# Two-layer conditional residual block on one core: TensorE's row loop begins at step 4, and two VectorE operations go behind a seven-product pair

## The chip, the cores and the metric

One core of one Trainium2 chip. The metric is device time in microseconds of one execution. Engines: PE (TensorE, matrix products; PEld is its weight loads), DVE (VectorE), ACT (ScalarE), POOL (GpSimd), SP (SyncE, which issues the DMAs).

## The reference

`x` is [8, 512, 256] in float32, `cond` [8, 8]. Layer 0 adds to each batch row the gated MLP of a shared expert and the two best of 8 experts (by `cond`, weights from a softmax); layer 1 adds a linear map with a low-rank part that depends on the row. Cut to what matters:

```python
def mlp(x, gate, up, down):                  # 256 -> 1024 -> 256
    return (gelu(x @ gate) * (x @ up)) @ down
w, sel = top_k(softmax(cond), 2);  w = w / w.sum()
x = x + sum(w[b, s] * mlp(x[b], *expert[sel[b, s]]) for s in range(2)) + mlp(x[b], *shared)
x = x + x @ W_base.T + b_base + 2 * sum_e cond[b, e] * (x @ As[e].T) @ Bs[e].T
```

## The kernel before

**Arithmetic.** Every float32 operand of PE is kept as two tensors: a high part (ACT writes it, `take_hi`, line 1086) and a remainder, the low part (DVE writes it, `take_lo`, line 1432). A product is three matmuls (high by high, high by low, low by high; `product`, line 757).

**Stages.** First the shared expert's MLP for all tokens (to about 250 us), then the routed experts and layer 1, one batch row after the other: `row(b, ...)` for b = 0 to 7 on each engine. A row has K = 16 steps, two for each 256 inner columns (a pair of steps) of the two experts. Pairs 1, 3, 5 and 7 (steps 2 and 3, 6 and 7, 10 and 11, 14 and 15; in row 0 only from step 6 on) form their gate and up parts by seven products of half the columns (`seven_products` on PE, `ex_seven` on DVE, from line 1691) in place of eight; they need sums of blocks of the weights and of the tokens, which POOL makes. The other pairs are whole steps.

**PE in a row.** At a whole step: gate (6 matmuls of 512 columns), up (6), the down part of two steps before (6). At a pair of seven: 42 matmuls of 256 columns, then two down parts (12 of 512). The last two down parts of a row are done in steps 0 and 1 of the next. Steps 4 and 8 carry layer 1 of the row before (12 matmuls) and the fold of the low-rank weights (6). The seventh product waits for `ex_v_done`, which DVE's line 1697 gives.

**DVE in a row.** At a whole step: gelu times up (line 1757), what is due at this step, the low part of the result, and more of what is due. At a pair of seven, `ex_seven`: lines 1697 and 1699 (add to copies of products), 1688, 1706, 1708, 1688 twice, then two low parts. What is due at a step is set by hand: `split_at` (the low part of a whole pair's weights, 1536 columns, line 1432), `sums_at` (of the sums of the weights), and constants. `T_STEP` = 13: `split_sums_x`, the low part of the next row's token sums. `W_EFF_STEP` = 9: line 1794 adds the folded weights, of PSUM, to the rest. Both come at a whole step just ahead of a pair of seven (14, 10). At step 14 the low part of the weights of the next row's pair 1 follows the seven.

**Order and loops.** Each engine runs its queue in program order, with semaphores between. On PE, ACT, DVE and SP row 0 is written out, rows 1 to 6 are a loop of three turns with two rows each, and row 7 is written out; POOL's loop has one row a turn. So each of PE, ACT and DVE jumps back twice, between rows 2 and 3 and between rows 4 and 5, and all of them at the same place of the program, the end of a row.

Of the kernel before, what the change touches and what calls it, by code (L numbers as in the profile page):

```python
# [5 lines left out]
ALU = mybir.AluOpType  # L6
# [29 lines left out]
def cond_resid_kernel(nc, x, cond, skill_gate, skill_up, skill_down, shared_gate, shared_up,  # L36
                      shared_down, w_base, b_base, lora_a, lora_b, out):
    B, S, H = x.shape
    E, _, I = skill_gate.shape
    R = lora_a.shape[1]  # L40
    HC = H // P
# [4 lines left out]
    K = TOP_K * IC  # L46
# [8 lines left out]
    COEF_STEP = 13  # L55
    FOLD_STEP = 8
    W_EFF_STEP = 9
    W_EFF_LO_STEP = 12
    X_STEP = 8
    T_STEP = 13  # L60


# [6 lines left out]
    with ExitStack() as ctx:  # L69
# [22 lines left out]
        w_id = sb("w_id", [P, HC * H])  # L92
# [25 lines left out]
        ps_misc = acc[1]  # L118
# [633 lines left out]
        def _(pe):  # L752
# [261 lines left out]
                    last = pe.transpose(ps_misc[1][:, o * P:(o + 1) * P], b_nat[:, o, :], ident[:])  # L1014
                last.then_inc(turned_w, 1)

            def row(b, par, first):
                pe.wait_ge(x_ready, b + 1)
                for k in range(K):
                    if k % 2 == 0:  # L1020
                        pe.wait_ge(weights_ready, b * (TOP_K * PAIRS) + k // 2 + 1)
                    if k // 2 in sevens_of(first):
                        if k % 2 == 0:
                            seven_products(b, par, k, SEVEN.index(k // 2), first)
                            if k == 2:

                                pe.wait_ge(x1_done, b * 2)
                            down(b, k - 2, first)
                            down(b, k - 1, first)
                        continue  # L1030

                    behind_seven = k // 2 - 1 in sevens_of(first) or (k < 2 and not first)
                    st = seventh(b, k, first)
                    if behind_seven:
                        if k % 2 == 0:
                            pe.wait_ge(ex_mul, 3 * st - 2)
                        else:
                            pe.wait_ge(ex_u1_done, st)
                    elif k >= 2:
                        pe.wait_ge(gelu_done, whole(b, k - 1, first))  # L1040
                    elif k == 0:
                        pe.wait_ge(sh_mul, 4 * (NU - 1) + 1)
                    else:
                        pe.wait_ge(u1_done, 2 * (NU - PAIRS))
                    project(par, k, ring[k % 2], GATE).then_inc(gate_done, 1)
                    if behind_seven:
                        pe.wait_ge(ex_c_done, 2 * st - 1 + k % 2)
                    elif k >= 2:
                        pe.wait_ge(mul_done, whole(b, k - 1, first))
                    else:  # L1050
                        pe.wait_ge(c_done, 4 * (NU - PAIRS) - 1 + k)
                    project(par, k, ring[2 + k % 2], UP).then_inc(up_done, 1)
                    if k == 1 and first:
                        shared_down_part(NU - 1, 0)
                        shared_down_part(NU - 1, 1)
                    if k < 2 and not first:

                        down(b - 1, K - 2 + k, False)
                    if k == 2:
                        pe.wait_ge(acc0_out, 2 * Q)  # L1060
                    if k >= 2:
                        down(b, k - 2, first)
                    if k == L1_STEP and not first:
                        layer1(b - 1)
                    if k == CONST_STEP and first:
                        pe.wait_ge(acc1_out, 2 * Q)
                        turn_constants()
                    if k == FOLD_STEP:
                        if first:
                            pe.wait_ge(w_turned, 1)  # L1070
                        else:
                            pe.wait_ge(o_ready, b * 2)
                        fold(b)

            row(0, 0, True)
            with pe.Fori(0, (B - 2) // 2) as i:
                row(i * 2 + 1, 1, False)
                row(i * 2 + 2, 0, False)
            row(B - 1, 1, False)
            down_last()  # L1080
            layer1_last()

# [345 lines left out]
        def _(dve):  # L1428
# [249 lines left out]
            def split_sums_x(b, par):  # L1678
                dve.wait_ge(ex_t_hi, b + 1)
                take_lo(sums_x(par, 1), t_tmp, sums_x(par, 0)).then_inc(ex_t_ready, 1)  # L1680
# [40 lines left out]
            def row(b, par, first, last):  # L1721
# [3 lines left out]
                def split_pair(pr):  # L1725
                    if pr < 2 * PAIRS:
                        split_routed(b, pr // PAIRS, pr % PAIRS, pr in sevens_of(first))
                    elif not last:
                        split_routed(b + 1, 0, pr - 2 * PAIRS, pr - 2 * PAIRS in SEVEN)

                def rest_of_x():
                    dve.wait_ge(x_hi, b + 2)
                    take_lo(x_cur(1 - par, 1), xf, x_cur(1 - par, 0)).then_inc(x_ready, 1)

                for k in range(K):
                    s = k // IC
                    if k // 2 in sevens_of(first):
                        if k % 2 == 0:
                            ex_seven(b, par, k, SEVEN.index(k // 2))
                            if k in split_at:  # L1740
                                split_pair(split_at[k])
                            if k == 2:
                                layer1_lo(b - 1)
                        continue
                    dve.wait_ge(gelu_done, whole(b, k, first) + 1)
                    dve.wait_ge(up_done, whole(b, k, first) + 1)
                    if k % 2 == 0 and (k // 2 - 1 in sevens_of(first) or (k == 0 and not first)):

                        dve.wait_ge(inner_ready, b * K + k)
                    if k == 0:  # L1750
                        if first:
                            dve.wait_ge(coef_done, 2)
                            V.tensor_copy(coef_now[:, 0, :], coef[:, 0, :]).then_inc(coef_ready, 1)
                        dve.wait_ge(coef_ready, b + 1)
                    if first and k < 2:
                        dve.wait_ge(sh_inner_hi, 4 * (NU - 1) + k + 1)
                    V.scalar_tensor_tensor(out=inner[k % 2], in0=gelu[k % 2], scalar=coef_now[:, par, s:s + 1],  # L1757
                                           in1=ring[2 + k % 2][:], op0=ALU.mult, op1=ALU.mult)\
                        .then_inc(mul_done, 1)

                    if k == L1_STEP + 1 and not first:
                        turn_output(b - 1)
                    if k == 1 and not first:

                        layer1_sum(b - 1)
                    if k == 4 and first:
                        split_sums_x(0, 0)
                    if k in sums_at:
                        split_sums_w(b, sums_at[k])
                    if k in split_at:  # L1770
                        split_pair(split_at[k])
                    if k == (BW_STEP if first else 0):
                        dve.wait_ge(bw_hi, b + 1)
                        V.scalar_tensor_tensor(out=bw_s[1], in0=b_t[:], scalar=coef_now[:, par, TOP_K:TOP_K + 1],
                                               in1=bw_s[0].bitcast(F32), op0=ALU.mult, op1=ALU.subtract)\
                            .then_inc(bw_ready, 1)
                    dve.wait_ge(inner_hi, b * K + k + 1)
                    take_lo(inner_s[1][:, k % 4, :], inner[k % 2], inner_s[0][:, k % 4, :])\
                        .then_inc(inner_ready, 1)
                    if first and k == 1:  # L1780
                        acc1_to_stage(Q - 1)
                    if k == L1_STEP and not first:
                        split_sums_w(b, 1)
                        split_pair(4)
                    if k == CONST_STEP and first:
                        layer1_constants()
                    if k == T_STEP and not last:
                        split_sums_x(b + 1, 1 - par)
                    if k == X_STEP and not last:
                        rest_of_x()  # L1790
                    if k == W_EFF_STEP:
                        dve.wait_ge(fold_done, b + 1)
                        dve.wait_ge(w_id_done, HC)
                        V.tensor_tensor(w_eff[:], ps_misc[0][:], w_id[:], ALU.add).then_inc(w_eff_done, 1)
                    if k == COEF_STEP and not last:
                        V.tensor_copy(coef_now[:, 1 - par, :], coef[:, b + 1, :]).then_inc(coef_ready, 1)
                    if k == W_EFF_LO_STEP:
                        dve.wait_ge(w_eff_hi, b + 1)
                        take_lo(w_eff_s[1], w_eff[:], w_eff_s[0]).then_inc(w_eff_ready, 1)
# [57 lines left out]
```

## Time and profile before

| | us |
|---|---|
| median of 3 runs | 809.85 |
| the three runs | 806.36, 809.85, 4542.35 |
| the profiled execution, whole time | 810.33 |
| its span, first to last instruction | 808.5 |
| mean granted TensorE clock, share of full | 0.995 |
| PE busy | 796.3 |
| DVE busy | 694.0 |
| ACT busy | 486.4 |
| POOL busy | 316.6 |

Times of the trace count from the span's start. "Idle before" names what ended an engine's idle time; "issue" means that nothing which the profile shows was waited for. Waits of some tenths appear with the weight loads and not with the matmuls, since a matmul still runs while the next load waits. The rows 1 to 7 of the batch begin at 317.94, 385.54, 455.64, 524.98, 595.02, 664.37 and 731.95 us by PE's first product.

### The profile page before, as it was taken

The numbers are of one execution on the slowest core, as the hardware profiler recorded it, in microseconds if no ns is written. First come the engines' busy times: TensorE is split into PE (matmuls) and PEld (weight loads), VectorE is DVE, ScalarE is ACT, GpSimd is POOL, SyncE is SP. The second block draws the span as 40 slices with busy tenths as digits, with TensorE's granted clock in tenths as the row PEclk, the third lists the DMA queues.
The fourth block names the chain that finished last, engine by engine and source line by source line (L and its number), as shares of the span: only waits on it lengthen the run. The fifth ranks groups of instructions, "written<-read, shape, count | busy, mean of one in ns | idle before, by whom it ended". The sixth has DMA issues, their size and how long they took to land.

```text
span 808.5 us, 13442 instructions
## 1 busy us (share of the span) xinstructions
PE 796.3 (98%) x4140; PEld 685.2 (85%) x4140; DVE 694.0 (86%) x916; ACT 486.4 (60%) x743; POOL 316.6 (39%) x308
## 2 busy tenths in 40 slices
PE   9999999999999999999999899999989999999998
PEld 7888888888888888888888789888878888898887
DVE  4886987987877899989989798998978999899886
ACT  6564554654654556666666566666756666675663
POOL 1441321321110773465246346425624632653520
PEclk9999999999999999999999999999999999999999
DMA  7340521303214422353163245316324522632400
GB/s 207 78 115 15 155 66 21 112 0 105 92 39 123 149 81 79 112 163 118 40 195 100 78 128 150 100 63 173 116 84 126 148 79 88 176 100 68 130 2 27
DMA packets 120160, 80.86 MB, mean 100 GB/s; under 512 B 62480, under 2 KB 115472, under 8 KB 120080
## 3 DMA queue, kind: packets, MB, share of 16 engines
q1 hardware_dynamic: 120080, 79.88, 33.9%
q8 instruction: 39, 0.64, 0.3%
q14 instruction: 41, 0.34, 0.1%
HBM read 67.28 MB, written 12.58 MB: 99 GB/s over the span
## 4 chain that ended last, share of the span: by engine, by line
PE 92%; DVE 5%; issue 2%; ACT 0%; POOL 0%; DVEq 0%; POOLq 0%; ACTq 0%
PE ps_ring L757 57%; PE ps_acc L757 33%; DVE inner_lo L1432 1%; DVE xc L1432 1%; DVE wide L1432 1%; PE ps_ring L877 1%; DVE post L1697 1%; DVE post L1757 0%; PE ps_acc L965 0%; DVE sh_dn L1432 0%; PE ps_acc L985 0%; PE ps_acc L871 0%; PE ps_ring L775 0%; DVE stage L1831 0%; ACT post L1322 0%
## 5 line engine op out<-in xcount | busy, mean ns | idle before, releaser
L757 PE MATMUL ps_ring<-xc,wide 128*128 128x512 f32 (+1 forms) x1938 | 421.9, 366 | 6.4 <-issue 4.6
L757 PEld LDWEIGHTS ps_ring<-xc,wide 128*128 128x128 f32 x1938 | 340.8, 189 | 68.2 <-issue 5.5
L1086 ACT CAST inner_hi<-post 128x512 fp32r<-128x512 f32 x192 | 117.7, 620 | 111.5 <-DVE post L1757 38.8
L757 PE MATMUL ps_acc<-inner_hi,wide 128*128 128x512 f32 x504 | 171.3, 390 | 0.0
L1432 DVE TENSOR_TENSOR inner_lo<-post,inner_hi 128x512 fp32r<-128x512 f32 x192 | 152.5, 802 | 8.6 <-ACT inner_hi L1086 5.7
L1089 ACT ACTIVATE post<-ps_ring 128x512 f32<-128x512 f32 (+1 forms) x125 | 67.8, 545 | 93.5 <-PE ps_ring L757 92.1
L757 PEld LDWEIGHTS ps_acc<-inner_hi,wide 128*128 128x128 f32 x504 | 94.9, 188 | 19.2
L757 PE MATMUL ps_acc<-inner_lo,wide 128*128 128x512 f32 x252 | 98.5, 391 | 0.0
L1089 ACT ACTIVATE post<-post 128x256 f32<-128x256 f32 (+1 forms) x98 | 53.8, 563 | 65.0 <-DVE post L1706 46.5
L637 POOL TENSOR_TENSOR post<-post 128x512 f32<-128x512 f32 x24 | 31.0, 1292 | 135.4 <-DVE post L1484 135.4
L757 PE MATMUL ps_acc<-inner_hi,sh_dn 128*128 128x512 f32 x256 | 83.9, 389 | 0.0
L1757 DVE SCALAR_TENSOR_TENSOR post<-post,coef_now,ps_ring 128x512 f32<-128x512 f32 x66 | 49.3, 746 | 30.1 <-PE ps_ring L757 29.1
L1432 DVE TENSOR_TENSOR wide<-raw,wide 128x1536 fp32r<-128x1536 f32 (+3 forms) x38 | 67.9, 1786 | 7.4 <-ACT wide L1086 7.4
L708 POOL TENSOR_TENSOR post<-post 128x256 f32<-128x256 f32 x62 | 44.5, 739 | 75.3 <-DVE post L1699 75.1
L716 POOL TENSOR_TENSOR post<-post 128x256 f32<-128x256 f32 x32 | 41.3, 1319 | 55.6 <-DMA post<-sh_scratch 55.6
L757 PE MATMUL ps_ring<-xc 128*128 128x256 f32 x456 | 62.3, 283 | 0.0
L1432 DVE TENSOR_TENSOR wide<-xbuf,wide 128x1536 fp32r<-128x1536 f32 x32 | 59.6, 1863 | 0.0
L757 PEld LDWEIGHTS ps_ring<-xc 128*128 128x128 f32 x456 | 58.1, 192 | 0.1
L757 PEld LDWEIGHTS ps_acc<-inner_hi,sh_dn 128*128 128x128 f32 x256 | 48.1, 188 | 10.0
L1086 ACT CAST wide<-raw 128x1536 fp32r<-128x1536 f32 (+3 forms) x40 | 52.3, 1308 | 4.8 <-DMA raw<-_L_cond_shared_gate_dram 3.7
L757 PEld LDWEIGHTS ps_acc<-inner_lo,wide 128*128 128x128 f32 x252 | 47.6, 189 | 8.8
L1432 DVE TENSOR_TENSOR xc<-stage,xc 128x1024 fp32r<-128x1024 f32 (+1 forms) x44 | 52.3, 1197 | 0.0
(128 smaller groups left out, 1040.4 us busy)
## 6 DMA issues: line engine op xcount, KB each, us to landing
raw<-n_L_cond_skill_gate_dram SPq DMA_DIRECT2D x32, 256.0 KB, 3.0
raw<-in_L_cond_skill_up_dram SPq DMA_DIRECT2D x32, 256.0 KB, 3.5
raw<-n_L_cond_skill_down_dram SPq DMA_DIRECT2D x32, 256.0 KB, 3.8
xbuf<-n_L_cond_skill_gate_dram SPq DMA_DIRECT2D x32, 256.0 KB, 3.0
xbuf<-in_L_cond_skill_up_dram SPq DMA_DIRECT2D x32, 256.0 KB, 3.5
xbuf<-n_L_cond_skill_down_dram SPq DMA_DIRECT2D x32, 256.0 KB, 3.7
xt_scratch<-xbuf SPq DMA_DIRECT2D x8, 512.0 KB, 3.1
sh_scratch<-stage SPq DMA_DIRECT2D x8, 512.0 KB, 2.7
```

The source lines that it names most:

```text
L637: G.tensor_tensor((g_t if part == GATE else i_t)[3], v57, u1, ALU.add).then_inc(c22_done, 1)
L708: last = G.tensor_tensor(ex_v[:, half], ex_v[:, half], ex_u1[:, half], ALU.add)
L716: done = G.tensor_tensor(base[:, part], base[:, part], xf[:, part], ALU.add)
L757: last = pe.matmul(dst, left_[a], right_[b], start=start and n == 0, stop=stop and n == len(PASSES) - 1, skip_group_check=adds)
L877: pe.transpose(ring[3][:, 0:P], ident[:], ident[:])
L1086: return nc.scalar.copy(dst, src)
L1089: return nc.scalar.activation(dst, src, ACT.Gelu_apprx_tanh)
L1432: return V.tensor_tensor(dst, src, hi.bitcast(F32), ALU.subtract)
L1697: V.tensor_tensor(ex_v, ring[3][:], ex_v, ALU.add).then_inc(ex_v_done, 1)
L1757: V.scalar_tensor_tensor(out=inner[k % 2], in0=gelu[k % 2], scalar=coef_now[:, par, s:s + 1], in1=ring[2 + k % 2][:], op0=ALU.mult, op1=AL ...
```

## The change

PE's loop is turned by four steps: the first four steps of row 1 are written out ahead of it, and the loop's last piece is the first four steps of the row after. The wait on `x_ready` goes to step 0 inside `row`. On DVE, `split_sums_x` moves from step 13 to behind `ex_seven` of step 14, ahead of the weights' remainder there; `fold_sum` (line 1794 with its waits) moves in row 0 from step 9 to behind `ex_seven` of step 10, and stays at step 9 in the other rows. ACT, POOL and SP are as before.

```diff
+    W_EFF_FIRST_STEP = 10
+    TURN_STEP = 4
...
-            def row(b, par, first):
-                pe.wait_ge(x_ready, b + 1)
-                for k in range(K):
+            def row(b, par, first, steps=range(K)):
+                for k in steps:
+                    if k == 0:
+                        pe.wait_ge(x_ready, b + 1)
...
             row(0, 0, True)
+            row(1, 1, False, range(TURN_STEP))
             with pe.Fori(0, (B - 2) // 2) as i:
-                row(i * 2 + 1, 1, False)
+                row(i * 2 + 1, 1, False, range(TURN_STEP, K))
                 row(i * 2 + 2, 0, False)
-            row(B - 1, 1, False)
+                row(i * 2 + 3, 1, False, range(TURN_STEP))
+            row(B - 1, 1, False, range(TURN_STEP, K))
...
+                def fold_sum():
+                    dve.wait_ge(fold_done, b + 1)
+                    dve.wait_ge(w_id_done, HC)
+                    V.tensor_tensor(w_eff[:], ps_misc[0][:], w_id[:], ALU.add).then_inc(w_eff_done, 1)
...
                             ex_seven(b, par, k, SEVEN.index(k // 2))
+                            if k == T_STEP + 1 and not last:
+                                split_sums_x(b + 1, 1 - par)
+                            if k == W_EFF_FIRST_STEP and first:
+                                fold_sum()
                             if k in split_at:
                                 split_pair(split_at[k])
...
-                    if k == T_STEP and not last:
-                        split_sums_x(b + 1, 1 - par)
...
-                    if k == W_EFF_STEP:
-                        dve.wait_ge(fold_done, b + 1)
-                        dve.wait_ge(w_id_done, HC)
-                        V.tensor_tensor(w_eff[:], ps_misc[0][:], w_id[:], ALU.add).then_inc(w_eff_done, 1)
+                    if k == W_EFF_STEP and not first:
+                        fold_sum()
```

## Rows read from the trace of the kernel before

**Rows 1.** The page, part 1: busy time of each engine.

```profile
PE 796.3 (98%) x4140; PEld 685.2 (85%) x4140; DVE 694.0 (86%) x916; ACT 486.4 (60%) x743; POOL 316.6 (39%) x308
```

**Rows 2.** Waits of PE and PEld: us in total, times, longest us.

```profile
PE ps_ring L757 <- issue: 4.6, 2, 2.4
...
PEld ps_ring L757 <- DVE post L1697: 3.7, 8, 1.7
```

**Rows 3.** Windows, rows 1, 2, 3, 7: length, busy (instructions), clock, DMA, GB/s.

```profile
317.94:385.54 67.60, 67.49 (x380) 59.22 (x378) 62.63 (x76) 44.30 (x64) 32.98 (x32) 1.00 0.40 118
385.54:455.64 70.10, 67.63 (x380) 59.03 (x378) 64.72 (x78) 44.90 (x65) 31.70 (x32) 1.00 0.38 114
455.64:524.98 69.34, 69.22 (x379) 60.45 (x379) 60.17 (x73) 43.65 (x63) 32.87 (x32) 0.98 0.39 115
...
731.95:799.17 67.22, 67.22 (x379) 59.15 (x378) 55.94 (x72) 40.21 (x61) 21.19 (x24) 1.00 0.19 52
```

**Rows 4.** Windows about PE's first jump and in row 0, same columns.

```profile
452.90:456.40 3.50, 1.15 (x5) 0.67 (x4) 3.26 (x4) 0.64 (x2) 0.00 (x0) 1.00 0.01 5
456.40:459.81 3.41, 3.41 (x9) 2.63 (x8) 0.00 (x0) 1.74 (x3) 0.00 (x0) 0.50 0.04 12
...
296.00:299.40 3.40, 1.92 (x15) 1.68 (x14) 3.40 (x6) 0.87 (x2) 1.97 (x3) 1.00 0.52 162
```

**Rows 5.** Timeline of PE where rows 2 and 3 begin: start, us, what.

```profile
385.54 2.88 PE L757 MATMUL ps_ring<-xc,wide 128*128 128x512 f32 x12
...
452.90 0.39 PE L757 MATMUL ps_acc<-inner_hi,wide 128*128 128x512 f32 x1
455.64 4.61 PE L757 MATMUL ps_ring<-xc,wide 128*128 128x512 f32 x12 [2.35 <-issue]
```

**Rows 6.** Timeline of DVE, row 1, steps 13 and 14.

```profile
380.03 1.21 DVE L1432 TENSOR_TENSOR xc<-stage,xc 128x1024 fp32r<-128x1024 f32 x1
...
381.24 0.68 DVE L1697 TENSOR_TENSOR post<-ps_ring,post 128x512 f32<-128x512 f32 x1
```

**Rows 7.** Timeline of PEld, the seventh product of step 14 in row 1.

```profile
381.97 0.78 PEld L757 LDWEIGHTS ps_ring<-sh_dn,wide 128*128 128x128 f32 x6 [0.31 <-DVE post L1697]
```

**Rows 8.** Timeline of DVE and PEld, row 0, steps 9 and 10.

```profile
296.91 0.68 DVE L1794 TENSOR_TENSOR w_eff<-ps_acc,w_id 128x512 f32<-128x512 f32 x1
297.51 0.67 DVE L1697 TENSOR_TENSOR post<-ps_ring,post 128x512 f32<-128x512 f32 x1
...
298.24 0.77 PEld L757 LDWEIGHTS ps_ring<-xc,wide 128*128 128x128 f32 x6 [1.68 <-DVE post L1697]
```

**Rows 9.** Timeline of DVE, then PEld, row 2, steps 0 to 4.

```profile
388.69 0.75 DVE L1757 SCALAR_TENSOR_TENSOR post<-post,coef_now,ps_ring 128x512 f32<-128x512 f32 x1
...
392.61 0.75 DVE L1757 SCALAR_TENSOR_TENSOR post<-post,coef_now,ps_ring 128x512 f32<-128x512 f32 x1 [0.49 <-PE ps_ring L757]
...
396.77 0.68 DVE L1697 TENSOR_TENSOR post<-ps_ring,post 128x512 f32<-128x512 f32 x1
...
402.45 1.22 DVE L1432 TENSOR_TENSOR sh_dn<-post,sh_dn 128x1024 fp32r<-128x1024 f32 x1
...
397.89 0.79 PEld L757 LDWEIGHTS ps_ring<-xc,wide 128*128 128x128 f32 x6
...
401.25 2.68 PEld L757 LDWEIGHTS ps_ring<-xc,wide 128*128 128x128 f32 x12
```

**Rows 10.** Instruction packets begun in 450.9:451.3, then in 454.3:455.4 (packets, MB, DMA share).

```profile
q8 instruction: 2, 0.03, 58.3%
...
q14 instruction: 2, 0.02, 4.3%
```

**Rows 11.** Timeline of DVE and ACT, the end of row 2 and row 3's step 0.

```profile
454.49 1.75 DVE L1432 TENSOR_TENSOR wide<-raw,wide 128x1536 fp32r<-128x1536 f32 x1
460.54 0.75 DVE L1757 SCALAR_TENSOR_TENSOR post<-post,coef_now,ps_ring 128x512 f32<-128x512 f32 x1 [4.30 <-PE ps_ring L757]
...
458.07 0.60 ACT L1089 ACTIVATE post<-ps_ring 128x512 f32<-128x512 f32 x1 [4.22 <-PE ps_ring L757]
```

## The prediction, made before the changed kernel was run

> **What bounds the kernel now.** I read the page first, then PE's waits and the row-by-row windows, then the timeline where those showed time missing. PE is busy for 796.3 of 808.5 us and DVE for 694.0 [rows 1], so PE is the bound, and only its idle or slowed time can be won. PE's own list of waits is short: two "issue" waits, 4.6 us together, and little else. The weight loads, which show shorter waits too, list 8 waits on DVE's line 1697, 3.7 us in all [rows 2]. The windows say which rows pay. Row 7, the last, takes 67.22 us, row 1 67.60, row 2 70.10 and row 3 69.34; rows 4, 5 and 6 repeat rows 2, 3 and 1 within 0.1 us [rows 3]. The work is the same in all but the last row's end, so three losses stand over 67.22:
> - 0.37 us in every row but the last (67.60 - 67.22, taken as the same 0.37 in all six rows from 1 to 6);
> - 2.50 us more in rows 2 and 4 (70.10 - 67.60), the pause at PE's jump back, of which 2.3 to 2.35 each is the "issue" wait;
> - 1.74 us in rows 3 and 5 (69.34 - 67.60), right behind it.
>
> The third is the clock: after 452.90 PE has 1.15 us of work in 3.50, then the granted clock is 0.50 for 3.41 us, and so again at the second jump [rows 4]. At half speed, 3.41 us holds 1.7 us of full-speed work, which is the 1.74. The first twelve products of row 3 take 4.61 us where row 2's take 2.88 [rows 5].
>
> **The change, part by part.**
> *(a) The token sums' remainder behind the seven products.* In row 1 DVE ends step 13 with the sums' remainder (380.03, 1.21 us), and only then comes line 1697 (381.24, 0.68 us), which PE's seventh product waits for [rows 6]. That product's loads start at 381.97, after 0.31 us of idle loads that line 1697 ends [rows 7]; the row's 0.37 is this wait. Without the remainder line 1697 starts at about 380.1 and ends near 380.8, 0.8 us before the loads are due at 381.6. All 0.37 goes, in six rows: 6 x 0.37 = 2.22. In row 0 the same wait is what the eight leave, 3.7 - 1.68 - 6 x 0.31 = 0.16 [rows 2, 7, 8], which I count as 0.2. Sum 2.4 us. What is late next there: ACT's and POOL's parts of the seven, which in steps 2 and 3 of every row run in this form with no wait of PE's, so nothing.
>
> *(b) The folded weights' sum in row 0.* Line 1794 starts at 296.91 and line 1697 at 297.51, so 0.60 us lies ahead of it; the seventh product's loads start at 298.24 after a wait of 1.68 [rows 8]. DVE is late from its earlier work too (line 1794 itself starts only at 296.91, when the loads had been due for 0.4), so only the 0.60 comes back and about 1.1 stays. The sum's readers are at step 12, far behind.
>
> *(c) What the remainder hits at its new place.* It now stands ahead of the 1.75 us weight remainder at the row's end, and so ahead of step 0 of the next row. I count from the next row's first product, B. In row 2 B is 385.54 [rows 5] and DVE's product of step 0 starts at 388.69 [rows 9], B + 3.15. Steps 2 and 3 of row 2 show a seven without a wait: step 4's loads start at 401.25, its product 0.23 later, and DVE is through with both low parts at 402.45 [rows 9], 0.97 behind. A row's last seven should now end so too: B + 0.97. The remainder (1.21) and the weight remainder (1.75 [rows 11], the two overlapping by 0.1) bring DVE's step 0 to B + 3.9, 0.7 later than now. From there DVE needs 3.3 us to step 1's product (388.69 to 392.61 less a wait of 0.49 and some overlap) and 4.84 more to the end of line 1697 (392.61 to 396.77 + 0.68). PE's seventh product is due at 397.89 [rows 9], B + 12.35. So step 0 may start as late as 12.35 - 4.84 - 3.3 = B + 4.2, and 3.9 is just in time. Price 0; past 4.2 each us costs PE one. The move issues no DMA itself. The remainder's own readers are PE's second product of step 2 (nearly 9 us behind B) and POOL's sums half a row on; SP's load into the slot that is freed at step 0 starts up to 0.7 us later, and its data is split at step 6, so nobody on PE's path waits for either. The bounds: 0, and 0.3 in each of seven rows if DVE's queue runs some tenths later than this count.
>
> *(d) PE's loop begins at step 4.* Products, loads and waits are the same in number; the back edge is still taken twice. Only its place moves: from behind the last seven and two down chunks to behind the first seven and two down chunks, that is, behind the same stream of 6 short and 12 long products. The pause is made so: both instruction packets of the queue that PE draws on start between 450.9 and 451.3 [rows 10], PE's products resume at 455.64, some 4.5 us later, and the work already queued lasts until 452.90 + 0.23 = 453.13 [rows 5]. With the same work queued ahead of the jump I expect the same pause, 2.5 us, twice. Zero gain is my value. The bounds: no pause at all (a gain of 4.9) and, upwards, a pause with nothing queued ahead (2 x 2.1 more). The second jump is the nearest row to the value: row 4 is within 0.1 of row 2. Half clock behind it: 2 x 1.74 now. It need not follow: in row 0 PE waits 1.68 us and the clock stays 1.00 [rows 4, 8]. A clock that stays up is worth 3.5 us, whichever place the jump has.
>
> The Trainium skill (Runtime: NRT & Kernel Launch, "Instruction fetch mechanics") says that a taken branch whose target is not among the pages held forces a fetch before execution goes on. By it the pause belongs to the branch and no place of the loop removes it; the packets of rows 10 agree. It speaks against the first part of the change and lowers the chance of rival 2. The skill (TensorE: Matmul & The Clock Gate, "Why this matters for your kernels") would keep the clock up over idle gaps as short as these. By it neither jump would be followed by half speed; the trace disagrees (0.50 behind both), and the measurement decides.
>
> *(e) Rows 3 and 5 begin without PE's pause.* Now DVE and ACT jump while PE pauses: DVE idles 4.30 us and ACT 4.22 before step 0 of row 3, both released by PE [rows 11]. After the change PE doesn't stop there, and their own jumps are bare. Two instruction packets, one for each, start within 454.3:455.4 [rows 10], I take ACT's as the first, since ACT was done first. With B at 453.13, ACT can't resume before B + 1.2, and does by 458.07, B + 4.9, which is 3.5 us behind a packet at 454.6. DVE taken as fast behind one at 455.1, resumes by 458.6, B + 5.5; its queued work lasts until B + 3.9, so its jump is hidden down to that. Bounds of the loss: 0, and 5.5 - 4.2 = 1.3 us in each of two rows. I take 0: the packets are early, and the ends of these idle times were set by PE.
>
> Sum: 2.4 + 0.6 = 3.0 us; the profiled execution took 810.33 (span 808.5), which gives 807.3. The median of the runs shown, 809.85, is 0.48 under it; the fastest, 806.36, is 3.5 under the median, which is what two spells of half clock cost. Against the median the forecast is 809.85 - 3.0 = 806.9.
>
> **Rivals.**
> 1. *The clock stays up behind both pauses* (the pauses fall elsewhere). For: 806.36 among the runs before. Against: both pauses seen were followed by 0.50. 806.9 - 3.5 = 803.4; 805.1 if one of the two.
> 2. *The pause shrinks or goes at the new place*, because the sequencer gets further ahead where the seventh product no longer waits. For: that wait stands ahead of the last seven's end, and so shortly ahead of the jump [rows 7]. Against: the stream queued behind it is the same. At most 4.9, with the clock 8.4; half a pause less and no slow spell gives about 801.
> 3. *DVE or ACT is late at steps 0 to 2 of rows 3 and 5* (part e), or of all rows (part c). At the bounds of (e), 2 x 1.3: 806.9 + 2.6 = 809.5.
> 4. *Slower than before.* The mechanism of 3 past its decisive point: the gain of 3.0 is used up when DVE starts step 0 of rows 3 and 5 later than B + 4.2 + 1.5 = B + 5.7. If DVE's jump began only when the weight remainder is done (B + 3.9) and took the 3 us of (e), it starts at 6.9: 2 x 2.7 = 5.4, so 809.85 - 3.0 + 5.4 = 812.3. Against: DVE's packet comes by 455.4, and DVE was at work until 454.49 + 1.75 = 456.24 [rows 10, 11].
> 5. *The moves do nothing*: another releaser holds the seventh product, 809.9. Against: row 7 has no remainder of the next row's sums, and it is the one without the 0.37.
>
> **How the numbers follow.** Forecast 0.53 (it includes small deviations of some tenths), rival 1 0.22, rival 2 0.08, rival 3 0.10, rival 4 0.04, rival 5 0.03. The time is the forecast's, 806.9. Range: down to 802.5, which takes in rival 1 and leaves out most of 2; up to 809.8, which takes in rival 3 and leaves out 4 and 5. A measurement can tell about 2%, 16 us, from no change. All of PE's losses together are 3.0 + 1.1 + 2 x (2.5 + 1.74) = 12.6, under 2%, so faster by that 0.01; rival 4 would need three times its price, so slower 0.01; within it 0.98.
>
> **What would show it.** Right: the 8 waits of loads on line 1697 become one, of about 1.1 us, in row 0; rows 1 and 6 last 67.2; the "issue" wait of some 2.4 us stands twice, now behind steps 2 and 3 of rows 3 and 5; DVE's first product of rows 3 and 5 starts near B + 3.9. Wrong: a pause under 2 us or over 3 (part d), PE waiting in steps 0 to 3 for lines 1757, 1697 or 1432 (parts c, e), or row 1 still at 67.6 (part a). The forecast fails as a whole if the clock is 1.00 throughout (then rival 1) or if rows 3 and 5 have lost over 1.5 us more in their first four steps.

## The result and the profile after

The changed kernel takes 799.53 us (median of 6 runs, 798.77 to 800.16) against 809.88 for the one before (6 runs): ratio 0.9883, 95% interval 0.9864 to 0.9902. Runs that came out far longer as a whole, here one of 4542.35 us of the kernel before, are left out of the ratios. That is 10.3 us less; the forecast was 3.0 less and a range down to 802.5. It falls outside. The moves on VectorE did about what was forecast. The jump of PE's loop, to which the forecast gave no change, stopped costing anything.

The page of the changed kernel (busy time, then the queue of PE's instruction packets):

```profile
PE 791.5 (99%) x4140; PEld 682.9 (86%) x4140; DVE 694.4 (87%) x916; ACT 486.3 (61%) x743; POOL 318.3 (40%) x308
...
q8 instruction: 21, 0.34, 0.2%
```

The page before has `q8 instruction: 39, 0.64, 0.3%`. The trace of before has 20 of these 39 from row 2 on (window 385.54:729):

```profile
q8 instruction: 20, 0.33, 0.4%
```

In the changed kernel the view of 452.44:722 has no q8 line at all. PE's waits after the change answer to [rows 2]:

```profile
PE ps_ring L880 <- POOL ident L609: 1.5, 1, 1.5
PE ps_ring L760 <- DVE post L1703: 1.0, 2, 0.9
PE ps_ring L760 <- DVE post L1772: 0.5, 1, 0.5
```

No "issue" wait is left (line 1703 is 1697 of before, 1772 is 1757, 760 is 757). The windows of rows 1, 2, 3 and 7 answer to [rows 3], same columns:

```profile
317.92:385.20 67.28, 67.28 (x379) 59.22 (x378) 62.31 (x75) 44.42 (x65) 32.73 (x32) 1.00 0.41 118
385.20:452.44 67.24, 67.24 (x380) 59.17 (x378) 62.02 (x75) 44.29 (x65) 32.09 (x32) 1.00 0.41 118
452.44:519.67 67.23, 67.23 (x379) 59.16 (x378) 62.65 (x75) 44.23 (x65) 32.43 (x32) 1.00 0.40 118
...
721.76:788.98 67.22, 67.22 (x380) 59.16 (x379) 56.05 (x72) 39.85 (x61) 21.22 (x24) 1.00 0.19 52
```

Each row takes 67.2 to 67.3 us and the clock is 1.00. Row 4 is the exception, 67.66, with a wait of the loads of 0.38 us at step 10. Against [rows 3], row 1 has lost 0.32 of its 0.37, row 2 also its 2.5, row 3 also its 1.74. Row 0 has gained nothing in this execution: row 1 begins at 317.92 us, before at 317.94. The new back edge lies in row 3 behind step 3. PE's timeline there:

```profile
467.92 0.39 PE L760 MATMUL ps_acc<-inner_lo,wide 128*128 128x512 f32 x1
468.15 0.39 PE L760 MATMUL ps_acc<-inner_hi,wide 128*128 128x512 f32 x1
468.38 0.84 PE L760 MATMUL ps_ring<-xc,wide 128*128 128x512 f32 x3
```

The last down product starts at 468.15 and the first of step 4 at 468.38: full pace across the jump, where [rows 5] show 2.35 us of idle time. The profiled spans, 808.5 and 798.3, differ by 10.2: 4.95 the two pauses (2.50 and 2.45 by the rows' lengths), 3.5 the two spells of half clock, 2.2 the waits of step 14 in rows 1 to 6, less 0.5 that rows 1 and 4 are longer than 67.2.

### The profile page after: what moved, and what is told of

The parts are those of the page before. It is cut to its first block, busy times and chain, and to the rows that moved or that the text cites. A ratio compares the mean times of both kernels' runs of the same rounds, so it can differ in the third digit from the quotient of the medians.

```text
span 798.3 us, 13454 instructions
## 1 busy us (share of the span) xinstructions
PE 791.5 (99%) x4140; PEld 682.9 (86%) x4140; DVE 694.4 (87%) x916; ACT 486.3 (61%) x743; POOL 318.3 (40%) x308
## 4 chain that ended last, share of the span: by engine, by line
PE 94%; DVE 4%; issue 2%; ACT 0%; DVEq 0%; POOL 0%; POOLq 0%
PE ps_ring L760 58%; PE ps_acc L760 34%; DVE xc L1438 1%; DVE inner_lo L1438 1%; PE ps_ring L880 1%; DVE wide L1438 1%; DVE post L1772 0%; PE ps_acc L968 0%; DVE post L1694 0%; PE ps_acc L988 0%; PE ps_acc L874 0%; DVE post L1703 0%; PE ps_ring L778 0%; DVE stage L1842 0%; PE ps_ring L782 0%
## 5 line engine op out<-in xcount | busy, mean ns | idle before, releaser
L1438 DVE TENSOR_TENSOR inner_lo<-post,inner_hi 128x512 fp32r<-128x512 f32 x192 | 149.8, 787 | 8.5 <-ACT inner_hi L1092 5.5
L1438 DVE TENSOR_TENSOR wide<-xbuf,wide 128x1536 fp32r<-128x1536 f32 x32 | 61.6, 1926 | 0.0
```

Source lines behind the costliest of these rows:

```text
L1438: return V.tensor_tensor(dst, src, hi.bitcast(F32), ALU.subtract)
```

## Experiments

What I looked for was a reason why the same jump, behind the same stream of products, costs 2.5 us in one kernel and nothing in the other. I counted the instructions of PE's program (a product is two, load and matmul): the loop of the kernel before stands at 2972 to 4592, that of the changed one at 3156 to 4780. A packet of q8 brings 16 KB, 0.64 MB in 39, and the stretches between packets in straight code are some 256 instructions. So 21 packets bring the program once, and 39 are 18 more, nine for each of the two jumps.
- **Theory A**: the loop's place among blocks of 256 instructions decides. PE holds a certain number of blocks; if the loop touches one too many, its start has been overwritten at the jump.
- **Theory B**: the step at which the loop turns decides.
- **Theory C** (rival 2 of the prediction): the pause went because the seventh product no longer waits ahead of the jump.

Each kernel ran beside the kernel before on one chip, and its ratio is to that. The kernel before took 809.8 us beside the two paddings by 82 and the two other turns, 809.2 beside the single parts and the padding of the kernel before by 45, 805.5 beside the padding of the changed kernel by 45, the move of pair 6 and the changed kernel once more, and 806.9 beside its own repetition. Only within such a group are times compared to less than that.

### The same loops, shifted by instructions that do nothing

```diff
             for u in range(1, NU):
+                for _ in range(11):
+                    pe.wait_ge(ident_ready, 1)
                 if u < PAIRS:
                     outputs(u, GATE)
```

The waits are met already, and cost PE nothing that shows: row 1 begins at 318.08 us in the padded kernel, at 317.94 in the one before. They stand at 15 places, 165 in all, which are 82 instructions of PE's program.

> The kernel before with 82 more PE instructions (waits that are met already, spread over 15 places of the shared stage), so that the unchanged loop stands 82 instructions further on in PE's program. No other work changes, and the loop still turns at the row's end. Theory A (what decides is where the loop lies in the blocks of 256 instructions that PE's instruction packets of 16 KB bring; the changed kernel's loop lies in 7 blocks, the one before in 8): now 7 blocks, no packets of q8 at the back edges, no pause, clock 1.00 throughout, 809.9 - 8.4 = 801.5 us. Theory B (the step at which the loop turns decides): pause and half clock as before, 809.9 us. Theory C (the pause went because the seventh product no longer waits): as before, 809.9 us.

Measured: 804.07 us (802.85 to 805.4), ratio 0.993 (0.9913 to 0.9947) to the kernel before. The instruction queue on this kernel's page:

```profile
q8 instruction: 21, 0.34, 0.2%
```

Its waits of PE:

```profile
PE ps_ring L757 <- DVE post L1699: 1.6, 2, 1.0
```

No issue wait, 21 packets, clock 1.00: the loop of before, turned at the row's end as before, has no pause once it is shifted. Theories B and C fall. The time is 2.6 us over the 801.5, so the pause is not all of it: rows 3 and 5 now have waits of 0.27 and 0.17 us of their own (part e), and row 1's wait at step 14 was 0.8 in this execution.

> The changed kernel with the same 82 instructions more ahead of the loop. Theory A: the loop now reaches into an eighth block, so the pause of 2.4 us is back at both back edges, now behind steps 2 and 3 of rows 3 and 5, with about 9 packets of q8 per turn; 799.5 + 4.9 = 804.4 us with the clock up, 807.9 us with half speed behind both. Theories B and C: 799.5 us, no pause.

Measured: 801.50 us (801.17 to 801.77), ratio 0.9894 (0.9877 to 0.991). The instruction queue on the page:

```profile
q8 instruction: 39, 0.64, 0.3%
```

PE's waits:

```profile
PE ps_ring L760 <- issue: 1.6, 2, 0.9
```

The same 82 instructions bring the pause back to the changed kernel, twice, with 39 packets. Its size was missed: PE's timeline shows 0.93 us at the first jump and 0.72 at the second, and the clock stays up.

```profile
466.76 0.39 PE L760 MATMUL ps_acc<-inner_hi,wide 128*128 128x512 f32 x1
468.08 1.18 PE L760 MATMUL ps_ring<-xc,wide 128*128 128x512 f32 x4 [0.93 <-issue]
```

### The turn at other steps

`TURN_STEP` = 2 and 6 in place of 4.

> The changed kernel with the loop turned at step 2 in place of 4. The loop starts at instruction 3045 of PE's program and ends at 4666, between the places of the two kernels. Theory A: 7 blocks as in the changed kernel, no pause, 799.5 us. Theory B, if it is step 4 that matters: a pause of some 2.4 us at each back edge, 804 to 808 us.

Measured: 799.04 us (2 runs, 797.95 and 800.12), ratio 0.9862 (0.9838 to 0.9887); 21 packets, no issue wait. Step 4 is nothing special.

> The changed kernel with the loop turned at step 6, still inside the row. It starts at instruction 3254 and ends at 4877. Theory A: an eighth block is touched, so the pause is back at both back edges, 804 to 808 us. Theory B (any place inside the row, away from the row's end, is free of it): 799.5 us.

Measured: 809.37 us (7 runs, 807.05 to 812.92), ratio 1.0002 (0.9983 to 1.0021). That is above the 804 to 808 of the expectation: all of the gain is gone, though both moves on VectorE are in. The instruction queue on the page:

```profile
q8 instruction: 39, 0.64, 0.3%
```

PE's waits:

```profile
PE ps_ring L760 <- issue: 5.8, 3, 2.9
```

These are three waits at two jumps: 0.60 and 2.28 us at the first, 2.89 at the second. The long ones stand five products behind the jump, not at it:

```profile
479.01 0.86 PE L760 MATMUL ps_ring<-xc,wide 128*128 128x256 f32 x5 [0.60 <-issue]
482.15 0.28 PE L760 MATMUL ps_ring<-xc,wide 128*128 128x256 f32 x1 [2.28 <-issue]
...
621.38 0.28 PE L760 MATMUL ps_ring<-xc,wide 128*128 128x256 f32 x1 [2.89 <-issue]
```

The loop starts at instruction 3254, and five products are ten instructions. A border between two blocks just behind the loop's start would make PE stop there, and "Where the border lies" puts one at 3255 to 3273 by another way.

### One part at a time

The moves alone have PE's loop as before; the turn alone has VectorE as before.

```diff
-            row(1, 1, False, range(TURN_STEP))
             with pe.Fori(0, (B - 2) // 2) as i:
-                row(i * 2 + 1, 1, False, range(TURN_STEP, K))
+                row(i * 2 + 1, 1, False)
                 row(i * 2 + 2, 0, False)
-                row(i * 2 + 3, 1, False, range(TURN_STEP))
-            row(B - 1, 1, False, range(TURN_STEP, K))
+            row(B - 1, 1, False)
```

> The two moves on DVE alone, PE's loop as before (1620 instructions in 8 blocks). Theory A: the pause and the half clock stay (clock 0.995), and only the waits on DVE go: 809.9 - 2.4 to 3.0 = about 807.2 us. Theory C (it is the seventh product's wait, ahead of the jump, that makes the pause): the pause is gone with it, 799 to 800 us.

Measured: 803.06 us, ratio 0.9944 (0.9914 to 0.9973), with ten runs from 800.12 to 808.28; the profiled one took 807.03. Its waits:

```profile
PE ps_ring L760 <- issue: 4.9, 2, 2.6
...
PE ps_ring L760 <- DVE post L1701: 0.9, 1, 0.9
```

Step 14 no longer waits and the pause is there, so C falls once more. The profiled execution is where the forecast stood (807.2). The median is lower, and the runs of the kernel before on that chip (803.21 to 811.62) spread as much. The run of 800.12 us has a clock of 1.00 and is within 0.6 us of the changed kernel: hardly any of the pauses' price is left in it. That the pauses are shorter or missing there is likely, but no such run was profiled.

> PE's turned loop alone, DVE as before. Theory A: no pause, clock 1.00, the waits on the seventh product of step 14 stay at 0.37 us in six rows; with the wait behind the bare jumps that the padded kernel showed (0.17 to 0.27 us in rows 3 and 5) it is within 1 us of that one's 804.1. If the parts simply add, 799.5 + 3.0 = 802.5 us.

Measured: 802.79 us (10 runs, 801.99 to 804.10 and one of 2050.21), ratio 0.9936 (0.9909 to 0.9962). No issue wait, 21 packets, and row 1 takes 67.57 as before. At row 3's start VectorE now shows its own jump:

```profile
454.90 1.75 DVE L1436 TENSOR_TENSOR wide<-raw,wide 128x1536 fp32r<-128x1536 f32 x1
458.00 0.75 DVE L1761 SCALAR_TENSOR_TENSOR post<-post,coef_now,ps_ring 128x512 f32<-128x512 f32 x1 [1.34 <-issue]
```

Row 3 begins at 453.54, so step 0 starts at B + 4.46, past the B + 4.2 of part (c), and PE loses 0.5 us in steps 2 and 3 of row 3 and 0.2 in row 5. The traces hold six such jumps of VectorE with no pause of PE's beside them, rows 3 and 5 of the turn alone and of the kernel before with 82 and with 45 instructions more. Step 0 starts there at B + 4.12, 4.16, 4.21, 4.21, 4.35 and 4.46, and the row is longer than 67.58 by 0.17, 0.21, 0.27, 0.26, 0.41 and 0.50. So each us past the limit does cost PE one, but the limit is B + 3.95 and not B + 4.2. In the changed kernel VectorE's timeline of the same place is:

```profile
453.33 1.22 DVE L1438 TENSOR_TENSOR sh_dn<-stage,sh_dn 128x1024 fp32r<-128x1024 f32 x1
454.47 1.75 DVE L1438 TENSOR_TENSOR wide<-raw,wide 128x1536 fp32r<-128x1536 f32 x1
456.14 0.74 DVE L1772 SCALAR_TENSOR_TENSOR post<-post,coef_now,ps_ring 128x512 f32<-128x512 f32 x1
```

and ScalarE's:

```profile
455.01 0.60 ACT L1095 ACTIVATE post<-ps_ring 128x512 f32<-128x512 f32 x1 [2.32 <-issue]
```

B is 452.44. The moved remainder (453.33) fills the time of VectorE's jump, step 0 starts at B + 3.70 with no idle time before it, and PE doesn't wait. ScalarE's jump does show, 2.32 us, and is early enough.

> The changed kernel with the folded weights' sum of row 0 back at step 9. My price for this move was 0.6 us: 799.5 + 0.6 = 800.1 us, with PE's wait at row 0's step 10 at 1.6 us or so in place of 1.0. If the lateness of DVE in row 0 comes from its operations beside POOL, which differ from run to run by as much, the difference isn't seen.

```diff
-    W_EFF_FIRST_STEP = 10
+    W_EFF_FIRST_STEP = 99
...
-                    if k == W_EFF_STEP and not first:
+                    if k == W_EFF_STEP:
```

Measured: 799.59 us (4 runs, 799.10 to 799.92), ratio 0.9898 (0.9842 to 0.9955). The interval is too wide to tell 0.6 us, and one pair of profiles doesn't tell it either: PE's wait on line 1703 in row 0 is 1.03 us here and 0.86 in the changed kernel, whose profile has one of 0.46 on line 1772 besides, and the spans are 797.5 and 798.3. All the profiles together do. PE's wait for that line at step 10 of row 0 is 1.03, 1.03, 1.46, 1.47, 1.47 and 1.48 us in the six with the sum at its old place, and 0.28, 0.44, 0.86, 0.86, 0.86, 0.87 and 0.87 in the seven with the sum moved and nothing else: 0.6 less in the mean. Row 1 begins at 318.08 us in the mean of the six and at 317.09 in that of the seven, but the two sets overlap.

### Where the border lies

> The kernel before with 45 instructions more ahead of PE's loop in place of 82: the loop starts at instruction 3017 of PE's program and ends at 4637. In the kernels without a pause it started at 3045, 3054 and 3156, in the one before at 2972. Theory A needs a border between two blocks somewhere from 2972 to 3045: with the border above 3017 the pause is back (two issue waits), below it there is none. Either outcome fits it; a pause of half the length does not.

Measured: 802.90 us (one run), 21 packets, no issue wait. The border is from 2973 to 3017.

> The changed kernel with 45 instructions more ahead of PE's loop in place of 82: the loop ends at instruction 4825. Theory A, made sharp: a loop without a pause has started at 3017 and ended at 4780, one with a pause has started at 2972; borders lie 256 instructions apart, so one lies between 2988 and 3017 and the one seven blocks on between 4780 and 4809. The end at 4825 is past it: the pause is back twice, some 1.1 to 2.5 us each, 9 packets of q8 per turn, 801 to 807 us. If what counts is only that the loop starts past some instruction, or its length, there is no pause and 799.5 us.

Measured: 800.18 us (799.04 to 802.94), ratio 0.9927 (0.9897 to 0.9958) on a chip where the changed kernel itself took 798.44. The instruction queue on this kernel's page:

```profile
q8 instruction: 30, 0.49, 0.3%
```

PE's waits:

```profile
PE ps_ring L760 <- issue: 1.8, 1, 1.8
```

Half right: the first back edge has the pause and a spell of half clock, the second has neither. The profiled run is the slowest of the six, 802.94; the other five are not profiled. All kernels together, by the place of the loop in PE's program:

| kernel | loop's instructions | q8 packets | issue waits |
|---|---|---|---|
| before, moves only | 2972 to 4592 | 39 | 2 |
| before + 45 | 3017 to 4637 | 21 | 0 |
| turn at step 2 | 3045 to 4666 | 21 | 0 |
| before + 82 | 3054 to 4674 | 21 | 0 |
| changed, turn only | 3156 to 4780 | 21 | 0 |
| changed + 45 | 3201 to 4825 | 30 | 1 |
| changed + 82 | 3238 to 4862 | 39 | 2 |
| turn at step 6 | 3254 to 4877 | 39 | 3, at 2 jumps |

With borders 256 apart, one between 2999 and 3017 and one seven blocks on between 4791 and 4809 put every row of the table right but for one back edge of "changed + 45", whose loop ends 16 to 34 instructions past the border. (3017 is where a free loop starts; 2999 follows from the turn at step 6, which lies in 8 blocks only if the next border, 256 on, is behind its start at 3254, and so at 3255 or later.) But for that edge, a loop free of the pause lies in 7 blocks, one with it in 8: of the 12 jumps of loops in 8 blocks that were profiled, 11 have the packets and the pause, of the jumps of loops in 7 blocks none. That the packets replace blocks which were overwritten is how I read it; the traces show the packets and not what PE holds.

### The rest of row 0, and both kernels again

```diff
+                            if k == 10 and first:
+                                split_pair(6)
                             if k in split_at:
                                 split_pair(split_at[k])
...
-                    if k in split_at:
+                    if k in split_at and not (k == 9 and first):
                         split_pair(split_at[k])
```

> The changed kernel, and in row 0 DVE's remainder of pair 6's weights (2.3 us at step 9) goes behind the seven of step 10 as well. PE's wait of 0.9 to 1.0 us on DVE's line 1703 in row 0 should go, if no later wait takes its place: 799.5 - 1.0 = 798.5 us. If DVE is then late at step 12, whose product needs this remainder, the same 799.5 us with the wait moved there.

Measured: 804.21 us (10 runs, 801.46 to 805.13 and one of 1610.29), ratio 0.9978 (0.9957 to 0.9999), 5.8 us slower than the changed kernel on the same chip. PE's wait:

```profile
PE ps_ring L760 <- DVE wide L1438: 3.5, 1, 3.5
```

The wait at step 10 is gone, and the second outcome is there, larger than written: step 12 waits 3.5 us for the remainder, and half clock follows (0.50 for 3.4 us from 304.2). So moves of this kind pay only while the moved operation's reader is far away.

> The changed kernel once more, beside the others on one chip: 799.5 us, no pause, 21 packets of q8.

Measured: 798.44 us (798.05 to 799.34), ratio 0.9918 (0.9887 to 0.9948), no pause, 21 packets. The gain is 7.0 us on this chip, not 10.3, and it is the kernel before that differs: 7 of its 15 runs here have a clock of 1.00 and take 803.79 to 805.50. The changed kernel's runs lie within 1.3 us of each other.

> The kernel before once more. Beside the last experiments its runs lay between 803.8 and 810.4 us, wider than half clock alone explains (3.5 us). It ends 39 to 68 instructions past a border. If the pause can be missing there at one back edge of the two, as in the changed kernel with 45 instructions more, some runs are near 810 and some near 804 to 806, and a profile may show one issue wait and 30 packets of q8. If the pause is certain (39 packets, two issue waits), the spread is the clock's alone and no run is under 806.

Measured: 809.07 us (10 runs, 804.65 to 812.08), ratio 1.0013 (0.9981 to 1.0046). The profiled execution, 812.08, has both pauses and 39 packets. The two runs with a granted clock of 1.00 took 804.65 and 805.09; those with 0.995 took 810.14 to 812.08. The 5 to 7 us between them is more than the 3.5 of half clock, and two runs are under 806, so the pause is not certain in full at both edges. A clock of 1.00 does not say how long a run takes: other runs of this kernel with it took from 802.74 to 808.99 us. Shorter pauses or one that is missing would explain it, but no such run was profiled, and the cause stays open.

## Why the prediction was wrong

- **Part (a), right.** 2.4 us forecast for step 14 of rows 0 to 6, 2.2 of it in rows 1 to 6. All of these but rows 1 and 4 last 67.2 us; row 1 keeps 0.06, and row 4 has a new wait at step 10. Line 1703 starts at 380.11 in row 1 where I had put 380.1. Of the 8 waits of loads two are left, 1.06 us in row 0 and 0.38 in row 4.
- **Part (b), right in size, but not seen in the changed kernel's own profile.** 0.6 forecast for the wait at step 10, and 0.6 is the mean difference over 13 profiles; the timed runs can't tell so little. In the profiled execution of the changed kernel it was used up: PE waited 0.46 us for line 1772 at step 10, which it had not done before and doesn't in the other profile of this kernel. What made VectorE late there was not tested.
- **Parts (c) and (e), right in their price.** Step 0 of row 3 was put at B + 3.9 (its terms, 0.97 + 1.21 + 1.75 - 0.1, make 3.83) and came at B + 3.70, and the price was 0 as forecast. ScalarE resumed at B + 2.57, far ahead of the B + 4.9 of part (e). The limit was too generous: it is B + 3.95 by the six jumps above, so there were 0.25 us to spare. Beside the turned loop the moves are worth 0.7 us more than parts (a) and (b) say, since without the remainder at the row's end VectorE's bare jump costs PE 0.5 us in row 3 and 0.2 in row 5.
- **Part (d), wrong, and it decided.** The step that failed reads "With the same work queued ahead of the jump I expect the same pause, 2.5 us, twice. Zero gain is my value." I worked out how much of a fetch is covered and took for granted that there must be a fetch. What the runs show in its place: the fetch itself depends on where the loop stands in the program. The turn at step 4 moved it on by 184 instructions, out of the eighth block, and no packet came at either jump. 82 instructions of padding did the same to the unchanged loop, and undid it in the changed one. The pause was worth 4.9 us and the clock behind it 3.5, which is the 8.4 that rival 2 named as its most, at a chance of 0.08 and for a reason that the experiments refute. The sign was in the trace of before: the prediction read the packets about the jump alone [rows 10], and not those of whole rows, 20 from row 2 on, which say that the loop is fetched anew in each turn.

The Trainium skill (Runtime: NRT & Kernel Launch, "Instruction fetch mechanics") was read one-sidedly. The prediction used its warning that a branch out of the pages held forces a fetch. The same section gives PE a store of 128 KiB, 2048 instructions, refilled in blocks of 256. By an estimate from these figures that is 8 blocks, and a loop can stay inside if it lies in 7 and the next block is fetched ahead. The runs agree: the changed kernel's loop of 1624 instructions has no packet of q8 from 451.13 to 736.24 us, over both of its jumps. The section also speaks of a window of two pages, 512 instructions, and with that the runs don't agree.

What was to show the forecast right or wrong did so: it named "a pause under 2 us" as the sign for part (d), and the pause was absent. It also named a clock of 1.00 throughout as the end of the forecast; that came true, though not by rival 1, in which the pauses stay.

## What to carry to other kernels

Before a back edge's pause is taken as the price of looping, look at whether instruction packets come at all during the turns, and count the loop's instructions: here a PE loop of 6.3 blocks of 256 ran free when it lay in 7 blocks and paused at 11 of 12 profiled jumps when it touched an eighth, and 45 instructions of padding, or a turn of the loop by some steps, were enough to go from one to the other. Such a gain is brittle: any edit ahead of the loop can lose it, so the place of the loop belongs among the things to look at after each edit. When one engine's jump gets cheap, the others' jumps, hidden beside it until then, become bare; an operation that isn't urgent, put just ahead of the loop's end, covered VectorE's here.

## What the runs showed of the hardware

- A jump back of PE with its target held costs nothing that the profile shows (468.15 to 468.38, the normal 0.23). With a fetch it cost 0.72 to 2.9 us of idle time in the profiles, with nine packets each time; what sets the length wasn't tested.
- The length of a pause alone doesn't say whether the granted clock falls to its lower level (0.50 of full). Those of 2.35 and 2.28 us in the profile of before were followed by 3.41 us at 0.50, as were 1.8 us in "changed + 45" and 2.6 us with the moves alone. Those of 0.93 and 0.72 us were not, and neither were the second one with the moves alone, 2.27 us (row 5 there lasts 67.36), nor the longest of all, 2.89 us in the turn at step 6.
- ScalarE's own jump shows as 2.32 us of idle time in row 3 of the changed kernel. VectorE's shows as 1.34 us behind a 1.75 us operation in row 3 with the turn alone, and as nothing where the moved remainder is queued ahead of it.
- At a border the outcome isn't sharp: with the loop's end 16 to 34 instructions past it, one back edge of two fetched in the one execution profiled.
